# Attention value products in six blocks of an iteration (3, 3, 2, 3, 3 and 2 key tiles) where eight blocks of 2 stood

## The chip, the cores and the metric

One Trainium2 chip, one core. The metric is the device time of one execution in microseconds, as a median of runs. Every number of the profile is from one profiled execution of the kernel.

## The reference

A transformer block with conditioned normalisation, for two sequences of 2048 tokens of width 512, in fp32:

```python
xm = _modulate(_ln(x), sh_msa, sc_msa)
q = (xm @ Wq + bq).reshape(B, S, NH, DH)      # B=2, S=2048, NH=16 heads, DH=32
k = (xm @ Wk + bk).reshape(B, S, NH, DH)
v = (xm @ Wv + bv).reshape(B, S, NH, DH)
q = q / DH
w = jnp.einsum('bqhc,bkhc->bhqk', q, k)
w = jax.nn.softmax(w, axis=-1)
y = jnp.einsum('bhqk,bkhc->bqhc', w, v).reshape(B, S, H)
x = x + g_msa[:, None, :] * (y @ Wo + bo)
xm2 = _modulate(_ln(x), sh_mlp, sc_mlp)
h = jax.nn.gelu(xm2 @ W1 + b1, approximate=False)
x = x + g_mlp[:, None, :] * (h @ W2 + b2)
```

## The kernel before

The program has three stages one after another: `project` (normalisation, q, k and v), `attend` (L754, the attention) and `feed_forward` (L1334). The change touches `attend` and three functions ahead of it.

Attention runs in `N_IT` = 32 iterations. One iteration is a group of `HPG` = 4 heads of one sequence and 512 queries; it goes over `NKT` = 16 key tiles of 128 keys. A key tile holds four scores, one for each head, so that an iteration has 64 scores. The same work lies on five engines, and each works through its own queue in the order written in the program:

- TensorE: for each head of each key tile one score product (`scores`, L1213, 97 rows, output 128 x 512 into one of three `s_bank`s), and behind each score one product for the row maxima of the next iteration (`max_product`, L1197, L1205 in rows). In iteration 0 there is one more of these for every eight scores (`maxima_issued`, L694). After every second key tile t (`t % 2 == 1`) it runs one block of value products (`times_v`, L1224): tiles t-3 and t-2, four heads each, into the one `y_bank`. A score or maximum uses the whole width of the array; a value product is 128 x 32, four of them side by side. The array thus changes between the two kinds at both ends of every block. Behind the block after key tiles 3 and 11 stand the denominators of an eight-tile half (`sums`, L1240, of the same 128 x 32 kind). At score 46, once an iteration, the maxima found are transposed into a row (`max_transpose`, L1208).
- VectorE: one reduction for every maximum product (`maximum`, L1075, L1078 in rows), then `negative` (L1080) and `as_row` (L1084) once an iteration.
- ScalarE: one exponential for every score (L1054) into `probs`, a ring of `RING` = 5 key tiles. Ahead of a tile's first exponential it waits in `slot_free` (L1035) until the value products of the tile five back are done, and until GpSimd has added up that tile's pair. `take_sum` (L987) copies the denominators out of their bank, `take_y` (L981) the value result.
- GpSimd: adds the probabilities of two tiles each (`first_pair`, L903, `second_pair`, L908) and issues the DMAs that fold them (`fold_quad`, `fold_half`).
- SyncE: loads keys, queries and values; `next_v` (L844) waits for the value products of a quarter before it loads the next group's.

The maximum products, the row and the denominators share one ring of four PSUM banks, handed out by `MaxRing` (L722) in the order of TensorE's queue. A product into a bank waits for the reader of what was there four uses before:

```python
            self.bank[use], self.count[use] = at % self.BANKS, counts[reader]
            after.append((reader, counts[reader]))
            self.free_after[use] = after[at - self.BANKS] if at >= self.BANKS else None
```

Likewise a score waits until the exponential three scores before it is done.

Of the kernel before, what the change touches and what calls it, by code (L numbers as in the profile page):

```python
# [18 lines left out]
HPG = P // DH  # L19
# [5 lines left out]
NKT = S // P  # L25
# [5 lines left out]
N_IT = B * G * BPB  # L31
N_MAX = BPB * HPG * TT
CHUNK = TOK // P
N_SC = HPG * NKT
N_TILES = N_IT * NKT
N_BLOCKS = N_TILES // 2
N_QUADS = N_TILES // 4
QPI = NKT // 4
LAST_QUAD = N_QUADS - QPI
# [2 lines left out]
LAST_HALF = LAST_QUAD // HALF_QUADS  # L42
# [11 lines left out]
class Space:  # L54


    def __init__(self, nc, ctx, name):
        self.parts = ctx.enter_context(nc.sbuf_tensor(f"{name}_parts", [P, KT, TOK], F32R))

        size = KT * TOK * 4  # L60
        self.plain = nc.alloc_sbuf_tensor_at(f"{name}_plain", [P, KT, TOK], F32, offset=nc.sbuf_base - size)
# [638 lines left out]
def maxima_at(i, s):  # L700

    return [(1 + g // N_MAX, g % N_MAX) for g in range(maxima_issued(i, s), maxima_issued(i, s + 1)) if 1 + g // N_MAX < N_IT]
# [4 lines left out]
    return i + 1 < N_IT and maxima_issued(i, s) <= N_MAX * (i + 1) + BEFORE - 1 < maxima_issued(i, s + 1)  # L707


def due_sums(b):  # L710

    if b >= N_BLOCKS - 3:
        first = LAST_HALF + b - (N_BLOCKS - 3)
        return (first - 1, first) if first == LAST_HALF else (first,)
    return ((b - 9) // 4,) if b >= 9 and b % 4 == 1 else ()


class MaxRing:  # L722
# [4 lines left out]
    def __init__(self):  # L727
        uses = []
        for i in range(N_IT):
            for s in range(N_SC):  # L730
                uses += [("max", j, n) for j, n in maxima_at(i, s)]
                if row_at(i, s):
                    uses.append(("row", i + 1))
                b, within = divmod(N_SC * i + s, 2 * HPG)
                if within == 2 * HPG - 1:
                    uses += [("sum", u) for u in due_sums(b) if u <= LAST_HALF]
        self.bank, self.count, self.free_after = {}, {}, {}
        counts = {"vector": 0, "scalar": 0}
        after = []
        for at, use in enumerate(uses):  # L740
            reader = "scalar" if use[0] == "sum" else "vector"
            counts[reader] += 1
# [3 lines that stand above are left out]
# [8 lines left out]
def attend(nc, sh, late, feed, x, Wo, W1, W2):  # L754
# [7 lines left out]
    with ExitStack() as ctx:  # L762
# [216 lines left out]
        @block.scalar  # L979
        def _(act):  # L980
            def take_y(i):  # L981
                act.wait_ge(av_done, NKT * (i + 1))
                if i >= 2:
                    act.wait_ge(y_stored, 16 * (i - 1))
                act.activation(y_buf[:, i % 2, :], y_bank[:, :], ACT.Copy).then_inc(y_taken, 1)

            def take_sum(h):  # L987
                act.wait_ge(d_done, h + 1)
                if h >= HPI and h % HPI == 0:
                    act.wait_ge(d_moved, 16 * h)  # L990
                act.activation(d_raw[:, h % HPI, :], m_bank[ring.bank["sum", h]][:, :], ACT.Copy).then_inc(d_taken, 1)

            def take_last_sums():
                act.wait_ge(d_done, LAST_HALF + QPI)
                act.wait_ge(d_moved, 16 * LAST_HALF)
                act.activation(d_raw[:, 0, :], m_bank[ring.bank["sum", LAST_HALF]][:, :], ACT.Copy).then_inc(d_taken, 1)

            def move_sums(i):
                act.wait_ge(d_taken, HPI * (i + 1))
                if i:  # L1000
                    act.wait_ge(small_ready, i)
                for q in range(HPI):
                    act.dma_start(d_small[:, q, :], d_raw[0:P:DH, q, :]).then_inc(d_moved, 16)

            def store_inv(i):
                act.wait_ge(small_ready, i + 1)
                if i:
                    act.wait_ge(inv_in, 16 * i)
                act.dma_start(sh.inv_rows, inv_small[:, :]).then_inc(inv_stored, 16)

            def load_inv(i):
                act.wait_ge(inv_stored, 16 * (i + 1))
                if i:
                    act.wait_ge(y_normed, i)
                act.dma_start(inv[:, :], sh.inv_rows.rearrange("h (a n) -> h a n", a=1).broadcast_to([HPG, DH, TOK])).then_inc(inv_in, 16)

            def store_y(i):
                group, tok = i // BPB, i % BPB * TOK
                act.wait_ge(y_normed, i + 1)
                act.dma_start(sh.y_cols[group, :, tok:tok + TOK], y_buf[:, i % 2, :]).then_inc(y_stored, 16)  # L1020

            def wo_high(t):
                act.wait_ge(feed.wo_in, 16)
                act.activation(feed.wo_hi[:, t, :], feed.wo_raw[:, t, :], ACT.Copy).then_inc(feed.wo_hi_ready, 1)

            def round_first_y(g):
                act.wait_ge(feed.y_in[g], 16)
                act.activation(feed.first_y_hi[:, g, :], feed.first_y[:, g, :], ACT.Identity, bias=sh.vecs[:, ROW_BV + g:ROW_BV + g + 1])

            def bias_first_y(g):  # L1030
                act.activation(feed.first_y[:, g, :], feed.first_y[:, g, :], ACT.Identity, bias=sh.vecs[:, ROW_BV + g:ROW_BV + g + 1]).then_inc(feed.y_biased, 1)

            SPARE = (7, 9, 11, 15)

            def slot_free(tile):  # L1035
                c, r = tile // 4, tile % 4
                act.wait_ge(av_done, tile + 1)
                if r == 0:
                    act.wait_ge(*firsts(c))
                if r == 2:  # L1040
                    act.wait_ge(second_ready, 2 * c + 2)

            for i in range(N_IT):
                for t in range(NKT):
                    tile = NKT * i + t
                    if t == 2 and i:
                        take_y(i - 1)
                    if tile >= 20 and tile % 8 == 4 and (tile - 20) // 8 < LAST_HALF:
                        take_sum((tile - 20) // 8)
                    for h in range(HPG):  # L1050
                        act.wait_ge(s_done, HPG * tile + h + 1)
                        if h == 0 and tile >= RING:
                            slot_free(tile - RING)
                        act.activation(probs[:, tile % RING, h, :], s_bank[(HPG * tile + h) % 3][:, :], ACT.Exp).then_inc(p_done, 1)  # L1054
                    if i >= 2:
                        if t == 1:
                            store_inv(i - 2)
                        if t == 5:
                            load_inv(i - 2)
                        if t == 13:  # L1060
                            store_y(i - 2)
                    if i and t == 13:
                        move_sums(i - 1)
                    if i == N_IT - 4 and t in SPARE:
                        wo_high(SPARE.index(t))
                    if i == N_IT - 3 and t in SPARE:
                        round_first_y(SPARE.index(t))
                    if i == N_IT - 2 and t in (3, 7, 9, 11):
                        bias_first_y((3, 7, 9, 11).index(t))
            take_y(N_IT - 1)  # L1070
            take_last_sums()
# [119 lines left out]
        def _(pe):  # L1191
# [114 lines left out]
            for i in range(N_IT):  # L1306
                pe.wait_ge(row_in[i % 2], 16 * (i // 2 + 1))
                for t in range(NKT):
                    for h in range(HPG):
                        scores(i, t, h)  # L1310
                        for j, n in maxima_at(i, HPG * t + h):
                            max_product(j, n)
                        if row_at(i, HPG * t + h):
                            max_transpose(i + 1)
                        n = N_SC * i + HPG * t + h - OUT_FROM
                        if 0 <= n < len(OUT_ORDER):
                            first_out(n)
                    if i == N_IT - 1 and t in (11, 13):
                        first_transposes(t - 11)
                        first_transposes(t - 10)  # L1320
                    if t % 2 == 1:
                        b = (NKT * i + t) // 2
                        if b:
                            times_v(2 * b - 2)
                            times_v(2 * b - 1)
                        for u in due_sums(b):
                            sums(u)
            first_up()
            times_v(N_TILES - 2)
            times_v(N_TILES - 1)  # L1330
# [438 lines left out]
```

## Time and profile before

| | us |
|---|---|
| median of 3 runs (2729.82, 2737.03, 2735.59) | 2735.59 |
| the profiled execution | 2730.14 |
| its span, first to last instruction | 2728.0 |
| attention: first score to last value product | 345.7 to 1920.4 |

Over the span TensorE is busy 2690.0 us, VectorE 2007.5, GpSimd 1870.5 and ScalarE 1341.3. Matmuls overlap in the array and their ends are modelled, so TensorE's busy time isn't a measure of how well it is used: the starts of its instructions are. In the rows below a line of the timeline is one or several like instructions in a row, with the time of the first start, the time to the end of the last, and in brackets the idle time of the engine ahead of them. A value product is recorded as two matmuls, so that `x16` is two key tiles.

### The profile page before, as it was taken

The numbers are of one execution on the slowest core, as the hardware profiler recorded it, in microseconds if no ns is written. First come the engines' busy times: TensorE is split into PE (matmuls) and PEld (weight loads), VectorE is DVE, ScalarE is ACT, GpSimd is POOL, SyncE is SP. The second block draws the span as 40 slices with busy tenths as digits, with TensorE's granted clock in tenths as the row PEclk, the third lists the DMA queues.
The fourth block names the chain that finished last, engine by engine and source line by source line (L and its number), as shares of the span: only waits on it lengthen the run. The fifth ranks groups of instructions, "written<-read, shape, count | busy, mean of one in ns | idle before, by whom it ended". The sixth has DMA issues, their size and how long they took to land. (4 is left out here: it accounts for less than half of the span.)

```text
span 2728.0 us, 37942 instructions
## 1 busy us (share of the span) xinstructions
PE 2690.0 (99%) x13737; PEld 1780.1 (65%) x13737; DVE 2007.5 (74%) x3326; ACT 1341.3 (49%) x2534; POOL 1870.5 (69%) x1083
## 2 busy tenths in 40 slices
PE   7999999999999999999999999999999999999998
PEld 5777755555555555555555555554788888888887
DVE  6557688888888888888888888887675765765754
ACT  2322267676676766767667676776221221221211
POOL 1000088989989999998999989897655455555553
PEclk9999999999999999999999999999999999999999
DMA  6555458788888879878888888875410110110000
GB/s 247 204 186 165 159 128 176 167 185 179 178 182 174 187 167 189 182 166 185 178 179 184 174 186 170 198 166 121 147 41 11 47 46 2 47 47 1 31 16 16
DMA packets 143754, 369.22 MB, mean 135 GB/s; under 512 B 23572, under 2 KB 40528, under 8 KB 119760
## 3 DMA queue, kind: packets, MB, share of 16 engines
q0 software_dynamic: 26784, 195.05, 35.8%
q1 hardware_dynamic: 96000, 155.26, 19.0%
q10 hardware_dynamic: 20784, 16.49, 2.1%
q8 instruction: 110, 1.80, 0.3%
q14 instruction: 76, 0.62, 0.1%
HBM read 111.97 MB, written 58.97 MB: 63 GB/s over the span
## 5 line engine op out<-in xcount | busy, mean ns | idle before, releaser
L1078 DVE TENSOR_REDUCE part_max<-shared_bank 128x1 f32<-128x512 f32 x1972 | 1207.3, 680 | 274.2 <-PE shared_bank L1205 274.1
L1054 ACT ACTIVATE probs<-s_bank 128x512 f32<-128x512 f32 x2048 | 1034.3, 627 | 289.0 <-PE s_bank L1221 285.2
L1232 PE MATMUL y_bank<-probs,vs 128*32 128x512 f32 x4096 | 493.2, 599 | 0.0
L905 POOL TENSOR_TENSOR first_sum<-probs 128x1024 f32<-128x1024 f32 x124 | 343.5, 2771 | 78.4 <-ACT probs L1054 78.3
L1655 ACT ACTIVATE h<-shared_bank,vecs 128x512 f32<-128x512 f32 x128 | 88.1, 688 | 562.9 <-PE shared_bank L1679 558.0
L1221 PE MATMUL s_bank<-late_parts 97*128 97x512 f32 x848 | 349.3, 413 | 2.5 <-ACT probs L1054 2.5
L905 POOL TENSOR_TENSOR half_sum<-probs 128x1024 f32<-128x1024 f32 x124 | 336.9, 2733 | 14.7 <-ACT probs L1054 14.6
L1205 PE MATMUL shared_bank<-late_parts 96*128 96x512 f32 x848 | 336.6, 397 | 0.9
L916 POOL TENSOR_TENSOR wo<-probs 128x1024 f32<-128x1024 f32 x124 | 335.0, 3063 | 0.4 <-ACT probs L1054 0.4
L916 POOL TENSOR_TENSOR second_sum<-probs 128x1024 f32<-128x1024 f32 x128 | 317.8, 2625 | 13.4 <-ACT probs L1054 6.4
L1465 POOL TENSOR_TENSOR late_parts<-w_raw,late_parts 128x512 fp32r<-128x512 f32 x96 | 129.2, 1346 | 226.3 <-DVE late_parts L1542 226.3
L1232 PEld LDWEIGHTS y_bank<-probs,vs 128*32 128x32 f32 x4096 | 106.9, 109 | 241.4 <-issue 121.7
L1221 PEld LDWEIGHTS s_bank<-late_parts 97*128 97x128 f32 x848 | 160.0, 189 | 133.5 <-issue 88.0
L1552 DVE CAST h_hi<-h 128x512 fp32r<-128x512 f32 x128 | 79.7, 623 | 179.2 <-ACT h L1655 179.1
L1677 PE MATMUL acc_bank<-w_hi,h_hi 128*128 128x512 f32 x512 | 201.4, 393 | 1.4 <-DVE h_lo L1554 1.3
L1677 PE MATMUL shared_bank<-late_parts 128*128 128x512 f32 x508 | 201.2, 396 | 1.1 <-PEq L762 1.1
L1679 PE MATMUL acc_bank<-w_hi,h_lo 128*128 128x512 f32 x512 | 200.8, 392 | 0.0
L1679 PE MATMUL shared_bank<-late_parts 128*128 128x512 f32 x508 | 199.3, 392 | 0.0
L1678 PE MATMUL acc_bank<-w_lo,h_hi 128*128 128x512 f32 x512 | 199.0, 389 | 0.0
L1678 PE MATMUL shared_bank<-late_parts 128*128 128x512 f32 x508 | 198.8, 391 | 0.0
L1205 PEld LDWEIGHTS shared_bank<-late_parts 96*128 96x128 f32 x848 | 161.4, 190 | 30.5 <-DVE part_max L1078 5.4
L1221 PE MATMUL s_bank<-space_parts,late_parts 97*128 97x512 f32 x432 | 177.7, 412 | 0.0
(199 smaller groups left out, 4566.8 us busy)
## 6 DMA issues: line engine op xcount, KB each, us to landing
half_sum<-second_sum POOLq DMA_DIRECT2D x62, 1024.0 KB, 13.5
first_sum<-wo POOLq DMA_DIRECT2D x62, 1024.0 KB, 10.0
half_sum<-first_sum POOLq DMA_DIRECT2D x62, 1024.0 KB, 7.6
late_plain<-in_x SPq DMA_DIRECT2D x16, 1024.0 KB, 7.0
q_parts<-qk_out SPq DMA_DIRECT2D x32, 512.0 KB, 3.1
k_parts<-qk_out SPq DMA_DIRECT2D x32, 512.0 KB, 3.4
late_parts<-q_parts SPq DMA_DIRECT2D x63, 256.0 KB, 11.4
late_parts<-k_parts SPq DMA_DIRECT2D x60, 256.0 KB, 11.8
```

Source lines behind the costliest of these rows:

```text
L905: pool.tensor_tensor(first_home(c)[:, hs, :], probs[:, 4 * c % RING, hs, :], probs[:, (4 * c + 1) % RING, hs, :], ALU.add).then_inc(first_ ...
L916: pool.tensor_tensor(second_home(c)[:, hs, :], probs[:, (4 * c + 2) % RING, hs, :], probs[:, (4 * c + 3) % RING, hs, :], ALU.add).then_inc ...
L1054: act.activation(probs[:, tile % RING, h, :], s_bank[(HPG * tile + h) % 3][:, :], ACT.Exp).then_inc(p_done, 1)
L1078: v.tensor_reduce(part_max[:, i % 2, hs, c:c + 1], m_bank[ring.bank["max", i, n]][:, :], AX.X, ALU.max).then_inc(m_taken, 1)
L1205: pe.matmul(m_bank[ring.bank["max", i, n]][:, :], queries[i % 3][0:STACK, h, s * P:(s + 1) * P], keys[u][0:STACK, h, :], start=True, stop= ...
L1221: pe.matmul(s_bank[n % 3][:, :], keys[u][0:STACK + 1, h, s * P:(s + 1) * P], queries[i % 3][0:STACK + 1, h, :], start=True, stop=True).the ...
L1232: last = pe.matmul(y_bank[h * DH:(h + 1) * DH, :], vs[:, t, h * DH:(h + 1) * DH], probs[:, tile % RING, h, :], start=(t == 0), stop=(t == ...
L1465: pool.tensor_tensor(feed.w1_lo(j), w1_raw[j * 4 // MT][:, :, j % (MT // 4) * P:(j % (MT // 4) + 1) * P], feed.w1_hi(j).bitcast(F32), ALU. ...
L1655: act.activation(h[:, j % 2, :], up_bank[j % 2][:, :], ACT.Gelu, bias=sh.vecs[:, ROW_B1 + j:ROW_B1 + j + 1]).then_inc(up_taken, 1)
L1677: pe.matmul(bank, hi_l, hi_r, start=first, stop=False)
L1678: pe.matmul(bank, hi_l, lo_r, start=False, stop=False)
L1679: return pe.matmul(bank, lo_l, hi_r, start=False, stop=last)
```

## The change

Value products are issued after the key tiles whose number less two is in `BLOCK_ENDS`, that is after tiles 4, 7, 9, 12 and 15 of an iteration and tile 1 of the next one, with 3, 3, 2, 3, 3 and 2 tiles a block. Before, it was after every odd tile, 2 tiles a block. The youngest tile of a block is two tiles back, as before. The last iteration keeps its blocks of two at the same places. The denominators stand behind the blocks after tiles 4 and 12 (before: 3 and 11), and ScalarE takes them ahead of the exponentials of tiles 5 and 13 (before: 4 and 12); `MaxRing` hands out the banks in that order. The last iteration keeps its denominators' places too.

```diff
-def due_sums(b):
-    if b >= N_BLOCKS - 3:
-        first = LAST_HALF + b - (N_BLOCKS - 3)
-        return (first - 1, first) if first == LAST_HALF else (first,)
-    return ((b - 9) // 4,) if b >= 9 and b % 4 == 1 else ()
+BLOCK_ENDS = (2, 5, 7, 10, 13, 15)
+
+def value_tiles(tile):
+    i, t = divmod(tile - 2, NKT)
+    if i == N_IT - 1:
+        return (tile - 3, tile - 2) if t % 2 == 1 else ()
+    if i < 0 or t not in BLOCK_ENDS:
+        return ()
+    at = BLOCK_ENDS.index(t)
+    first = BLOCK_ENDS[at - 1] + 1 if at else 0
+    return range(NKT * i + first, NKT * i + t + 1)
+
+def due_sums(tile):
+    i, t = divmod(tile, NKT)
+    if i == N_IT - 1:
+        return {3: (LAST_HALF - 2,), 11: (LAST_HALF - 1, LAST_HALF), 13: (LAST_HALF + 1,), 15: (LAST_HALF + 2,)}.get(t, ())
+    return ((tile - 20) // 8,) if tile >= 20 and tile % 8 == 4 else ()
...
-                b, within = divmod(N_SC * i + s, 2 * HPG)
-                if within == 2 * HPG - 1:
-                    uses += [("sum", u) for u in due_sums(b) if u <= LAST_HALF]
+                if s % HPG == HPG - 1:
+                    uses += [("sum", u) for u in due_sums(NKT * i + s // HPG) if u <= LAST_HALF]
...
-                    if tile >= 20 and tile % 8 == 4 and (tile - 20) // 8 < LAST_HALF:
-                        take_sum((tile - 20) // 8)
+                    for u in due_sums(tile - 1) if tile else ():
+                        if u < LAST_HALF:
+                            take_sum(u)
...
-                    if t % 2 == 1:
-                        b = (NKT * i + t) // 2
-                        if b:
-                            times_v(2 * b - 2)
-                            times_v(2 * b - 1)
-                        for u in due_sums(b):
-                            sums(u)
+                    for tile in value_tiles(NKT * i + t):
+                        times_v(tile)
+                    for u in due_sums(NKT * i + t):
+                        sums(u)
```

## Rows read from the trace of the kernel before

**Rows 1.** The page: busy time, share of the span and instructions of each engine.
```profile
PE 2690.0 (99%) x13737; PEld 1780.1 (65%) x13737; DVE 2007.5 (74%) x3326; ACT 1341.3 (49%) x2534; POOL 1870.5 (69%) x1083
```
**Rows 2.** Iteration 14: window, length, busy (instructions) of PE, PEld, DVE, ACT, POOL.
```profile
1030.07:1078.78 48.71, 48.63 (x277) 27.33 (x274) 39.70 (x68) 33.78 (x67) 43.40 (x24) 1.00 0.88 185
```
**Rows 3.** Timeline of TensorE around one block of value products.
```profile
1003.18 0.39 PE L1205 MATMUL shared_bank<-keys,late_parts 96*128 96x512 f32 x1
1003.50 1.92 PE L1232 MATMUL y_bank<-probs,vs 128*32 128x512 f32 x16
1005.35 0.50 PE L1221 MATMUL s_bank<-late_parts 97*128 97x512 f32 x1
1005.69 0.39 PE L1205 MATMUL shared_bank<-keys,late_parts 96*128 96x512 f32 x1
...
1008.94 0.40 PE L1205 MATMUL shared_bank<-keys,late_parts 96*128 96x512 f32 x1
```
**Rows 4.** Timeline of TensorE around a block with denominators behind it.
```profile
1036.20 0.40 PE L1205 MATMUL shared_bank<-late_parts,space_parts 96*128 96x512 f32 x1
...
1039.48 0.39 PE L1205 MATMUL shared_bank<-late_parts,space_parts 96*128 96x512 f32 x1
1039.80 1.92 PE L1232 MATMUL y_bank<-probs,vs 128*32 128x512 f32 x16
...
1042.51 0.50 PE L1221 MATMUL s_bank<-late_parts 97*128 97x512 f32 x1
```
**Rows 5.** Timeline of VectorE: the eight reductions behind the block of rows 3.
```profile
1006.12 4.88 DVE L1078 TENSOR_REDUCE part_max<-shared_bank 128x1 f32<-128x512 f32 x8 [0.92 <-PE shared_bank L1205]
```
**Rows 6.** Timeline of TensorE's weight loads at the end of that block.
```profile
1005.35 0.19 PEld L1221 LDWEIGHTS s_bank<-late_parts 97*128 97x128 f32 x1 [0.84 <-issue]
1005.46 0.19 PEld L1205 LDWEIGHTS shared_bank<-keys,late_parts 96*128 96x128 f32 x1
```
**Rows 7.** Timeline of all engines, a stretch of iteration 0 with nine maxima.
```profile
360.19 5.47 DVE L1078 TENSOR_REDUCE part_max<-shared_bank 128x1 f32<-128x512 f32 x9 [0.71 <-PE shared_bank L1205]
...
363.02 0.81 PE L1205 MATMUL shared_bank<-late_parts 96*128 96x512 f32 x2
363.32 0.19 PEld L1205 LDWEIGHTS shared_bank<-late_parts 96*128 96x128 f32 x1 [0.34 <-DVE part_max L1078]
363.76 0.16 PEld L1232 LDWEIGHTS y_bank<-probs,vs 128*32 128x32 f32 x8 [0.25 <-ACT probs L1054]
```
**Rows 8.** Timeline of all engines around the row of maxima, end of key tile 11.
```profile
1014.55 1.88 DVE L1078 TENSOR_REDUCE part_max<-shared_bank 128x1 f32<-128x512 f32 x3
...
1014.72 0.48 PE L1221 MATMUL s_bank<-late_parts 97*128 97x512 f32 x1
1015.28 0.19 PEld L1205 LDWEIGHTS shared_bank<-late_parts,space_parts 96*128 96x128 f32 x1 [0.40 <-DVE part_max L1078]
...
1016.34 0.27 DVE L1088 CAST neg_max_row<-shared_bank 16x128 fp32r<-16x128 f32 x1
1016.54 0.67 DVE L1078 TENSOR_REDUCE part_max<-shared_bank 128x1 f32<-128x512 f32 x1
```
**Rows 9.** Timelines of GpSimd and of ScalarE, iteration 10: pair 4, 5; tiles 8, 9.
```profile
857.68 3.06 POOL L905 TENSOR_TENSOR first_sum<-probs 128x1024 f32<-128x1024 f32 x1
...
859.74 4.03 ACT L1054 ACTIVATE probs<-s_bank 128x512 f32<-128x512 f32 x8 [1.77 <-PE s_bank L1221]
```
**Rows 10.** Who waited for whom in the whole span, with times and longest.
```profile
PEld s_bank L1221 <- issue: 212.1, 253, 0.8
...
PEld shared_bank L1205 <- DVE part_max L1078: 14.8, 39, 0.4
```
**Rows 11.** The same for ScalarE alone, from 394 us to 1870 us.
```profile
ACT probs L1054 <- POOL first_sum L905: 0.9, 1, 0.9
```

More of the change, by code:

```diff
@@ L35 @@
 N_TILES = N_IT * NKT
-N_BLOCKS = N_TILES // 2
 N_QUADS = N_TILES // 4
```

## The prediction

> **What bounds the kernel now.** I read the page first, for how much each engine has to do: TensorE is busy 99% of the span, VectorE 74%, GpSimd 69%, ScalarE 49% [rows 1]. Then one iteration by itself, since the change alters 31 of the 32 alike: of 48.71 us TensorE is busy 48.63, GpSimd 43.40, VectorE 39.70, ScalarE 33.78, all at the full granted clock [rows 2]. TensorE carries the end, and every other engine has some room on the average. But the change leaves the averages nearly alone and alters the order in time, so the timelines decide.
>
> The first thing to see in them is what a block of value products costs besides its products. From the last maximum ahead of a block to the first one behind it are 2.51 us, 1003.18 to 1005.69 [rows 3]. A step between two scores or maxima is 3.25 / 14 = 0.232 us there and 3.28 / 14 = 0.234 in the other stretch [rows 3, 4]; I take 0.2335. With the denominators (one key tile's worth of the same products) last maximum to next score takes 1042.51 - 1039.48 = 3.03 us, against 1005.35 - 1003.18 = 2.17 without [rows 3, 4], so a tile is 0.86 us, and the denominators pay for no change of their own. Of the 2.51 us, 2 x 0.2335 are steps and 2 x 0.86 are products: 0.33 us is the price of turning the array to the narrow products and back. It shows as a gap of 0.84 us ahead of a score's weight load [rows 6], 253 times in the waits [rows 10], some eight times an iteration.
>
> The second thing is VectorE between two blocks. It takes a reduction every (4.88 - 1.88) / 5 = 0.600 us, 0.68 us each [rows 5, 8], while TensorE makes a maximum every 0.467 us. It loses 0.133 us per maximum and makes it good during the value products; its 0.92 us idle ahead of the next eight [rows 5] shows that it does.
>
> **What the change removes.** Two turns of the array in each of iterations 0 to 30: 62 x 0.33 = -20.5 us. The same 16 value tiles and two denominators are made, at 0.86 us each, in both orders. Before and after, the denominators share a turn with value products. This is on TensorE's path and comes off whole, if nothing else is late.
>
> **What it adds: runs of 12 maxima where runs of 8 stood.** The runs between blocks become 12, 12, 8, 12, 12 and 8 (tiles 2-4, 5-7, 8-9, 10-12, 13-15, 0-1). The ring of four banks lets a maximum start only when the reduction of the one four before is over. Let a run start at 0 with its first score (1005.35). Its first maximum is at 0.34 and the k-th after it at 0.34 + 0.467k [rows 3]; its weight load, where nothing holds it, starts one step earlier, at 0.11 + 0.467k (1005.46 for the first [rows 6]). The reductions start at 0.77 (1006.12) and the k-th ends at 1.45 + 0.60k [rows 5]. The load of maximum k+4 is free about 0.05 us later: in iteration 0, where a run has nine maxima, the fifth reduction ends at 360.19 + 4 x 0.599 + 0.68 = 363.27 and the ninth maximum's load starts at 363.32 [rows 7].
>
> So the eighth maximum (k = 7) could be loaded at 3.38 and is free at 1.45 + 1.80 + 0.05 = 3.30. Runs of eight fit by 0.08 us, and that is why the waits show VectorE holding such a load 39 times only [rows 10]: 30 rows of maxima and nine in iteration 0. The ninth is free at 3.90 and wants 3.84, and each further one is 0.133 later. A late load isn't hidden: from 363.32 to the block behind are 0.44 us, from an unhindered maximum 0.32 [rows 3, 7], and a score behind a gap comes 0.34 before the next instead of 0.2335 [rows 3], so some 0.11 us of it shows. The twelfth (k = 11) therefore starts at 1.45 + 0.60 x 7 + 0.05 + 0.11 = 5.81 instead of 0.34 + 5.14 = 5.48. **A run of 12 is 0.33 us longer**: exactly what a saved turn gives back. The small delays of the ninth to eleventh are contained in it, for the last one alone sets when the block starts. There are three such runs.
>
> The fourth, tiles 10 to 12, has the row of maxima in it. Up to its eighth maximum, which today already waits (load at 1015.28 [rows 8]), nothing changes. Behind it: the next score streams at 1015.28 + 0.11 + 0.23 = 1015.62, and its maximum must wait for the second of the three reductions from 1014.55, which ends at 1014.55 + 0.60 + 0.68 = 1015.83: with 0.05 and 0.11 that is 1015.99, where 1015.86 was possible. The next waits for the third, 1016.43 + 0.16 = 1016.59 instead of 1016.46. The last two wait for the copy of the row, over at 1016.61, and for the reduction over at 1017.21 [rows 8], and both are in time. Together 0.26 us.
>
> Sum of an iteration: 3 x 0.33 + 0.26 - 2 x 0.33 = **+0.58 us**. Iterations 1 to 29: +16.8. Iteration 0 has 13, 14, 13 and 14 maxima in the long runs, nine in the two short ones. By the same terms a run of nine loses 0.17 (4.01 against 3.84), one of 13 loses 6.41 - 5.71 = 0.70, one of 14 loses 1.07. Eight nines lose 1.4 now; four long runs and two nines 3.9 after: +2.5 - 0.66 = +1.8. In iteration 30 the maxima end at key tile 10, so only two long runs are late: 0.66 - 0.66 = 0. The last iteration keeps its blocks. In all +18.6 us on the profiled execution's own 2730.1 (span 2728.0): 2748.7. The profiled execution was 5.5 us under the median of the runs; on the median the sum is 2735.6 + 18.6 = **2754.2 us**.
>
> **Moved steps, costed at nothing.** ScalarE's scores ring of three banks: its eight exponentials take 4.03 us [rows 9], 0.50 apart at most against 0.467, so a run of 12 costs it 0.4 us of lead at most, while the maxima's waits give TensorE's scores as much back. `take_sum` moves one tile later with its denominators, still directly behind them; the DMA of the denominators (tile 13) comes behind it as before. `slot_free` wants the value products of five tiles back: with a block after tile 4 tile 5 finds tile 0 done, since its score stands behind that block on TensorE anyway. On SyncE's queue `next_v` waits for tile 3's and tile 11's products, two tiles later each; the first row load stands behind tile 7's products, whose block (after tile 9) doesn't move. Those loads have most of an iteration. GpSimd: the pair of tiles 4 and 5 must be added before tile 9's exponentials. In iteration 10 it ends at 860.74 and tile 9 begins at 859.74 + 4 x 0.467 = 861.61, 0.9 us later [rows 9]; this is one of the closest, and held up by a fold's DMA that starts with tile 1 and so moves with tile 1. Where nothing holds it the room is about 2.8 us and shrinks by 0.8. It held ScalarE once for 0.9 us in 30 iterations [rows 11]. Bound: 0 to +3 us in all; I take 0.
>
> **Bounds of the added cost.** With the release lag at nothing a run of 12 loses 0.28, with 0.10 it loses 0.38; with a period of 0.595 it loses 0.30, 0.605 gives 0.37. Four runs in 30 iterations: 0.05 us each way is 6 us. A turn may be 0.31 to 0.35, 1.2 us each way. So +11 to +26, and the runs shown spread over 7 us.
>
> **The rivals.**
> (a) *Turns saved and nothing late*: 2735.6 - 20.5 = 2715 us. For it speaks that VectorE idles in every iteration [rows 2, 5]. Against it are the waits of rows 7 and 8, where the ring holds TensorE already with one maximum more than eight. The Trainium skill ("TensorEngine Tiling (Array Packing)", Key Properties) says that a change of tiling mode drains the engine; by that rule alone fewer blocks are all gain. The same page (Performance Considerations, PSUM Bottleneck) says that tiling speeds up TensorE but not the emptying of PSUM, which may become the bottleneck; that speaks for my forecast, and rows 7 show it. Chance 0.08.
> (b) *A draw*: the late loads cost about half of what I work out (the exposed 0.11 us already lies in the turn behind the run, so that a run loses 0.22 and the one with the row 0.15): 3 x 0.22 + 0.15 - 0.66 = +0.15 us an iteration, +5 us, 2740; with the low bounds above 0 or a little below. Against it is the 0.44 us of rows 7, which contains the entry to the block. Chance 0.14.
> (c) *GpSimd becomes late too*: its pair decides where its room, 0.9 us at the closest, falls under 0. If that came to 1 us in every iteration, 31 us more: about 2785. Against it the rows 9 and 11. Chance 0.04.
> (d) *A turn is not saved*: a block of three pays its third tile's own 0.33, and only the waits are added: 2735.6 + 18.6 + 20.5 = 2775. The denominators' 0.86 us as a third tile [rows 4] speak against it. Chance 0.03.
> The forecast has 0.71.
>
> **How the numbers follow.** About 0.3%, 8 us, is what a measurement of this kernel can tell from no change. The likeliest case gives 2754, with its bounds 2747 to 2762 on the median; a spread of some 5 us between medians of three runs makes that 2741 to 2767, which also holds part of the draw and leaves under 0.2 outside. Slower has the forecast, (c) and (d): 0.78. Within 0.3%: 0.14. Faster: 0.08.
>
> **What would show it.** In the windows an iteration takes 49.3 us. The block of three lasts 2.71 us from its first product to the next score, with the denominators 3.57. In the waits, the weight load of the maxima held by VectorE rises from 39 to several hundred (three or four in each long run), and the gap of 0.84 us falls from 253 to about 190. The twelfth maximum of an undisturbed run starts its load 5.70 us after the run's first score. I am wrong if an iteration is 48.1 us (a), or if ScalarE waits for GpSimd dozens of times (c).

## The result, and the profile after

| | before | after |
|---|---|---|
| median of the runs, us | 2735.55 (4 runs, 2729.82 to 2737.03) | 2772.14 (4 runs, 2770.53 to 2774.76) |
| ratio, 95% interval | | 1.014 (1.0124 to 1.0156) |
| profiled execution, us | 2730.14 | 2771.92 |
| its span, us | 2728.0 | 2769.8 |

The change makes the kernel 1.4% slower, where 0.7% slower (+18.6 us) was forecast. By the medians the loss is 36.6 us, by the two profiled executions 41.8, since the one of the kernel before was 5.5 us under its median. The sign and one mechanism were right, and about half of the loss wasn't in the sum. The page of the changed kernel, busy time by engine (as rows 1), then its iteration 14 (as rows 2: window, length, busy time of PE, PEld, DVE, ACT and POOL):

```profile
PE 2709.2 (98%) x13737; PEld 1763.9 (64%) x13737; DVE 2003.3 (72%) x3326; ACT 1350.2 (49%) x2534; POOL 1868.0 (67%) x1083
```
```profile
1050.29:1100.30 50.01, 49.23 (x277) 26.93 (x273) 39.59 (x68) 34.06 (x67) 44.24 (x24) 1.00 0.88 185
```

No engine has more to do. An iteration takes 50.01 us instead of 48.71, and TensorE now stands still for 0.8 us of it. To place the 41.8 us that the two spans differ by, the same stretches of both: iteration 0, iterations 1 to 29 together, iteration 30. First the kernel before, then the changed one.

```profile
345.68:396.76 51.08, 50.99 (x249) 30.37 (x250) 44.70 (x74) 33.85 (x65) 46.26 (x25) 0.93 0.53 114
...
396.76:1810.58 1413.82, 1410.26 (x7922) 793.07 (x7918) 1150.68 (x1971) 984.11 (x1951) 1283.27 (x670) 1.00 0.84 179
...
1810.58:1858.73 48.15, 47.75 (x274) 26.60 (x270) 34.32 (x51) 36.17 (x71) 47.11 (x26) 1.00 0.77 168
```
```profile
347.34:399.74 52.40, 51.68 (x249) 27.83 (x249) 44.25 (x74) 35.38 (x65) 45.66 (x25) 0.97 0.51 110
...
399.75:1850.71 1450.96, 1427.28 (x7921) 779.93 (x7917) 1147.83 (x1970) 991.65 (x1951) 1284.48 (x670) 1.00 0.83 174
...
1850.71:1903.08 52.37, 49.98 (x273) 26.88 (x269) 34.61 (x51) 36.46 (x71) 45.39 (x25) 0.97 0.70 153
```

| stretch | forecast, us | measured, us |
|---|---|---|
| ahead of the first score (345.68 to 347.34) | 0 | +1.7 |
| iteration 0 | +1.8 | +1.3 |
| iterations 1 to 29 | +16.8 (0.58 each) | +37.1 (1.28 each) |
| iteration 30 | 0 | +4.2 |
| the rest | 0 | -2.5 |

The 1.7 us ahead of the first score aren't the change's. The execution of the changed kernel has 3.4 us at half clock in the first stage, and that of the kernel before hasn't (the changed one, then the one before; the number ahead of the DMA's two is the granted clock):

```profile
40.50:43.90 3.40, 3.40 (x13) 3.01 (x14) 3.29 (x7) 2.00 (x4) 0.00 (x0) 0.50 0.35 130
...
40.50:43.90 3.40, 3.40 (x20) 2.83 (x19) 3.26 (x8) 2.10 (x4) 0.00 (x0) 1.00 0.37 141
```

Of the runs further on, e2, e8 and e9 have the same spell and their first score at 346.98, 347.34 and 347.52 us; e4 and e7 haven't, and are at 345.49 and 345.99.

The open question is thus 0.70 us in each of 29 iterations. The runs between the blocks answer where. This is the timeline of the changed kernel's run of tiles 2 to 4 in iteration 14, TensorE, its weight loads and VectorE, as rows 3, 5 and 7:

```profile
1056.09 0.50 PE L1239 MATMUL s_bank<-late_parts 97*128 97x512 f32 x1
...
1056.87 7.27 DVE L1096 TENSOR_REDUCE part_max<-shared_bank 128x1 f32<-128x512 f32 x12 [0.60 <-PE shared_bank L1223]
...
1061.80 0.19 PEld L1223 LDWEIGHTS shared_bank<-late_parts,space_parts 96*128 96x128 f32 x1 [0.30 <-DVE part_max L1096]
1062.22 0.16 PEld L1250 LDWEIGHTS y_bank<-probs,vs 128*32 128x32 f32 x8 [0.24 <-issue]
```

The twelfth maximum's load starts 1061.80 - 1056.09 = 5.71 us behind the first score; 5.70 was forecast. The reductions are (7.27 - 0.68) / 11 = 0.599 us apart. From first score to block the run takes 6.13 or 6.14 us in each of iterations 1 to 29, where an unhindered one would take 5.48 + 0.32 = 5.80. The run 5 to 7 takes 6.14 (once 6.21), the run with the row 6.73 instead of 4.59 for its eight. The two kinds of delay that were worked out are there, at their sizes. The run of tiles 13 to 15 is another matter: 6.88 us, 1.08 more than unhindered. TensorE in it, iteration 14:

```profile
1090.72 0.50 PE L1239 MATMUL s_bank<-late_parts,keys 97*128 97x512 f32 x1
...
1093.88 0.39 PE L1223 MATMUL shared_bank<-space_parts,late_parts 96*128 96x512 f32 x1
1094.96 0.50 PE L1239 MATMUL s_bank<-late_parts,keys 97*128 97x512 f32 x1 [0.69 <-ACT probs L1072]
...
1097.59 2.78 PE L1250 MATMUL y_bank<-probs,vs 128*32 128x512 f32 x24
```

One score starts 1.08 us behind the product ahead of it, 0.85 more than a step, for ScalarE. It is the last of tile 14, and by the ring of three score banks it waits for the exponential of the first of tile 14. ScalarE's own timeline tells why that one is late:

```profile
1091.35 1.57 ACT L1072 ACTIVATE probs<-s_bank 128x512 f32<-128x512 f32 x3
1092.67 0.32 ACTq L1037 DMA_DIRECT2D y_cols<-y_buf  x1
1092.78 0.63 ACT L1072 ACTIVATE probs<-s_bank 128x512 f32<-128x512 f32 x1
1093.08 1.13 ACTq L1020 DMA_DIRECT2D d_small<-d_raw  x2
1094.31 4.03 ACT L1072 ACTIVATE probs<-s_bank 128x512 f32<-128x512 f32 x8 [0.90 <-PE s_bank L1239]
```

Behind tile 13's exponentials its queue issues three DMAs (`store_y` and the two of `move_sums`, "if t == 13"), 0.32 and 1.13 us; the store's issue and the start of the others still lie under the last exponential. From 1093.41 to 1094.31 no exponential runs, though their scores are long there. The bracket names TensorE as the releaser, which had been done; by the order of the rows, what held ScalarE is the issuing row above it, and e1, e2 and e9 test that. Before the change the same issues stood ahead of a block of value products:

```profile
1022.26 0.32 ACTq L1020 DMA_DIRECT2D y_cols<-y_buf  x1
...
1022.68 1.13 ACTq L1003 DMA_DIRECT2D d_small<-d_raw  x2
1024.77 4.03 ACT L1054 ACTIVATE probs<-s_bank 128x512 f32<-128x512 f32 x8 [1.69 <-PE s_bank L1221]
```

They were over at 1023.81, about a microsecond before the next score gave ScalarE anything to do.

Iteration 30 has the same kind of loss once more, behind key tile 11, where `bias_first_y` has its last operation. The first product of the output projection (L1302, behind the first score of tile 12) needs it, and a block no longer stands between. TensorE idles 1.12 us, and its granted clock, full until then, is at 0.50 (1.2 GHz) in the next 3.4 us. The timeline and the window:

```profile
1886.58 0.47 PE L1302 MATMUL shared_bank<-space_parts,late_parts 128*128 128x512 f32 x1 [1.12 <-ACT late_plain L1048]
```
```profile
1887.10:1890.50 3.40, 3.40 (x14) 1.72 (x16) 3.40 (x1) 1.79 (x3) 3.40 (x2) 0.50 0.39 77
```

The kernel before had such a window in its last iteration, 1902.2 to 1905.6 at 0.50, and the changed one hasn't; part of the 2.5 us given back there lies in that. The stall doesn't settle whether the clock falls: e9 has it too, in the same place and of the same 1.12 us, and its clock stays at 1.00 behind it. Its product and window:

```profile
1864.76 0.47 PE L1303 MATMUL shared_bank<-space_parts,late_parts 128*128 128x512 f32 x1 [1.12 <-ACT late_plain L1051]
```
```profile
1865.20:1868.60 3.40, 3.40 (x27) 1.50 (x29) 3.40 (x1) 1.57 (x3) 3.40 (x2) 1.00 0.63 161
```

The waits of the whole span: the ring of the maxima held a load 39 times before and does 207 times now (several hundred was forecast; e9, with the issues out of the way, has 288); the gap ahead of a score behind a block fell from 253 to 191 times (about 190 was forecast). Not forecast is the growth of the second row below, scores held by exponentials: 239 times and 80.3 us, where it was 25 times and 11.8 us before.

```profile
PEld s_bank L1239 <- issue: 160.1, 191, 0.8
...
PEld s_bank L1239 <- ACT probs L1072: 80.3, 239, 1.3
PEld shared_bank L1223 <- DVE part_max L1096: 60.8, 207, 0.4
```

### The profile page after: what moved, and what is told of

It reads as the page before. It is cut to its first block and busy times, and to the rows that moved or that the text cites. A ratio compares the mean times of both kernels' runs of the same rounds, so it can differ in the third digit from the quotient of the medians.

```text
span 2769.8 us, 37942 instructions
## 1 busy us (share of the span) xinstructions
PE 2709.2 (98%) x13737; PEld 1763.9 (64%) x13737; DVE 2003.3 (72%) x3326; ACT 1350.2 (49%) x2534; POOL 1868.0 (67%) x1083
## 5 line engine op out<-in xcount | busy, mean ns | idle before, releaser
L1250 PE MATMUL y_bank<-probs,vs 128*32 128x512 f32 x4096 | 480.2, 597 | 0.0
L922 POOL TENSOR_TENSOR first_sum<-probs 128x1024 f32<-128x1024 f32 x124 | 335.2, 2703 | 146.2 <-ACT probs L1072 146.2
L922 POOL TENSOR_TENSOR half_sum<-probs 128x1024 f32<-128x1024 f32 x124 | 345.5, 2794 | 10.5 <-ACT probs L1072 10.4
L1223 PE MATMUL shared_bank<-late_parts 96*128 96x512 f32 x848 | 346.6, 409 | 1.0
L1250 PEld LDWEIGHTS y_bank<-probs,vs 128*32 128x32 f32 x4096 | 113.3, 109 | 253.4 <-issue 196.7
```

The lines of the kernel that those rows point to most:

```text
L922: pool.tensor_tensor(first_home(c)[:, hs, :], probs[:, 4 * c % RING, hs, :], probs[:, (4 * c + 1) % RING, hs, :], ALU.add).then_inc(first_ ...
L1223: pe.matmul(m_bank[ring.bank["max", i, n]][:, :], queries[i % 3][0:STACK, h, s * P:(s + 1) * P], keys[u][0:STACK, h, :], start=True, stop= ...
L1250: last = pe.matmul(y_bank[h * DH:(h + 1) * DH, :], vs[:, t, h * DH:(h + 1) * DH], probs[:, tile % RING, h, :], start=(t == 0), stop=(t == ...
```

## The experiments

**e1, the issues behind tile 15.** Theory: ScalarE's issues (the store and the move of the denominators) are the missing 0.75 us. Rival: the ring of the maxima or GpSimd makes the run 13 to 15 long.

```diff
-                        if t == 13:
+                        if t == 15:
                             store_y(i - 2)
-                    if i and t == 13:
+                    if i and t == 15:
                         move_sums(i - 1)
```

> The changed kernel, with ScalarE's two DMA issues (the store of the normalised values and the move of the denominators) behind key tile 15 instead of 13. Theory: behind tile 13 they now stand inside a run of twelve scores, hold up the exponentials of tile 14 and through the three score banks TensorE; behind tile 15 a block of value products covers them. Then the run of tiles 13 to 15 falls from 6.88 us to the 6.14 of the other long runs, an iteration from 50.03 to 49.3 us, and the time from 2772 to about 2750. Rival, VectorE or GpSimd make that run long: nothing changes, 50.0 us an iteration, 2772.

Measured: the run 13 to 15 takes 6.12 to 6.14 us in iterations 1 to 29, as the theory has it, and iteration 1 takes 49.27 us. But the kernel takes 3164.58 us, 1.160 times the time of the kernel before (1.1581 to 1.1615). The waits, then iteration 1:

```profile
DVE d_total L1111 <- DMA d_small<-d_raw: 420.2, 31, 26.0
...
ACT y_buf L1002 <- DVE inv_small L1115: 392.9, 30, 20.5
```
```profile
399.16:448.43 49.27, 49.16 (x277) 27.24 (x273) 39.20 (x66) 33.89 (x67) 41.59 (x23) 1.00 0.75 154
```

VectorE waits for the moved denominators at score 3 of the next iteration (`invert_small`), up to 26 us, its reductions stand in the queue behind, and the ring holds TensorE. ScalarE stands as well, since the store of the reciprocals behind tile 1 of its queue waits for them (the second row). In the kernel before, VectorE's wait was 1.8 us in all. A part of the loss is the clock: the mean granted clock of this execution is 0.934, against 0.998 in the kernel before beside it. The issue can't simply go where a block covers it: what it moves is due. The time of this run says nothing about the question; the runs and the iteration free of the new wait do.

**e2, the same cost in the kernel before.** The same issues behind key tile 12, inside a run of two tiles (`13` replaced by `12` in the lines of e1's diff).

> The kernel before, with the same two issues behind key tile 12 instead of 13, so that they stand inside a run of two tiles instead of ahead of a block. Theory: the fourth score of tile 13 waits about 0.8 us for the exponential of the first, the run 12 to 13 goes from 3.94 to 4.8 us, an iteration from 48.72 to 49.5 and the time from 2735 to about 2760. Rival, the issues cost nothing in any place: 48.72 and 2735.

Measured: ratio 1.0116 (1.0101 to 1.0131), 2760.71 us; the run 12 to 13 takes 4.95 us in most iterations (mean 4.99) instead of 3.94, an iteration 49.75:

```profile
1083.74 1.13 ACTq L1003 DMA_DIRECT2D d_small<-d_raw  x2
1085.00 2.07 ACT L1054 ACTIVATE probs<-s_bank 128x512 f32<-128x512 f32 x4 [0.94 <-PE s_bank L1221]
```
```profile
1085.65 0.50 PE L1221 MATMUL s_bank<-late_parts,keys 97*128 97x512 f32 x1 [0.69 <-ACT probs L1054]
```

The same three kinds of rows as in the changed kernel, without any change of blocks or maxima: the issues inside a run cost 1.0 us an iteration. That is more than the 0.8 expected. In the changed kernel they make the run 1.08 us longer than unhindered too, and 0.33 us of that lies over the delay that the ring of the maxima would cause by itself, so that they add 0.75 there. How it divides between the store and the move wasn't tried.

**e3 and e4, reductions of half the length.** They take VectorE's lag away, to see what the blocks do alone; half of the keys is left out of the maxima. e3 is e1's kernel, e4 the one before, both with this edit:

```diff
-                v.tensor_reduce(part_max[...], m_bank[...][:, :], AX.X, ALU.max)
+                v.tensor_reduce(part_max[...], m_bank[...][:, 0:TOK // 2], AX.X, ALU.max)
```

> The kernel of e1, with each of VectorE's reductions of the maxima over 256 of the 512 columns; the other half of the keys is left out of the maxima. Theory: the reductions then keep up with the maxima, the long runs lose their 0.34 us each, and what is left of the change is the saved turns: 2 x 0.33 us an iteration less than the kernel of e4, about 47.7 against 48.4 us. Rival, the exponentials (0.48 to 0.49 us apart against 0.467) hold the long runs: they stay 6.14 us and an iteration stays within 0.3 us of e1's 49.3.

> The kernel before with the same half reductions (256 of 512 columns, half of the keys left out of the maxima), as the counterpart of e3. Both theories: the runs of eight stay at 3.93 to 3.96 us; only the one with the row of maxima shortens from 4.59 by some 0.3 us, an iteration from 48.72 to about 48.4, the time to about 2726.

Measured: e3 takes 3118.12 us, for e1's reason, and only its runs can be used: 5-7 at 5.95, 10-12 at 5.97 and 13-15 at 5.88 us where e1's were 6.13, 6.73 and 6.13. e4: ratio 0.9955 (0.9939 to 0.9972), an iteration at 48.24 us, all of it from the run with the row of maxima: 4.06 us instead of 4.59. So the ring and VectorE's lag make the long runs longer, by 0.18 to 0.25 us more than the exponentials would by themselves (6.13 - 5.95 and 6.13 - 5.88).

**e5, e6: SyncE issues the move.** The way to free ScalarE without a late landing of the denominators. `move_sums` itself is moved to SyncE's program as it is; e6 has the half reductions besides.

```diff
                 load_row(i + 1)
+                if i:
+                    move_sums(i - 1)
...
-                        if t == 13:
+                        if t == 15:
                             store_y(i - 2)
-                    if i and t == 13:
-                        move_sums(i - 1)
```

> The changed kernel with both issues out of ScalarE's way without a later landing: SyncE issues the move of the denominators, behind the row's load and as soon as they are taken (key tile 13), and ScalarE stores the normalised values behind tile 15. In e1 the move behind tile 15 landed too late for the reciprocals at score 3, which held VectorE and then everything; its iteration 1, in which no reciprocals are due, took 49.27 us. Theory (the issues were the 0.75 us an iteration that the sum had missed; late landing was all that was wrong in e1): run 13 to 15 at 6.13 us, every iteration at 49.3, the time 0.56 us x 30 = 17 us above the kernel before and 22 below the changed one. Rival (the maxima's ring or GpSimd lengthen that run in the steady state): 50.0 us.

> The kernel of e5 with VectorE's reductions over 256 of the 512 columns, so that half of the keys is left out of the maxima. Against e4 (48.24 us an iteration). If VectorE's reductions are all that lengthens the long runs, an iteration is 0.67 us under e4's, 47.57 us. If the exponentials hold them for 0.1 to 0.15 us each, as e3's runs show, it is 47.75 to 47.9. If the turns saved are worth nothing, it is 48.2 or more. Time: 14 us under e4's by the middle case.

Measured: e5 1.062 (1.0599 to 1.0642), e6 1.0472 (1.0446 to 1.0497). The run 13 to 15 is at 6.13 us again, but the run 2 to 4 takes 11.5 us on average from iteration 3 on, with spells of half clock in most iterations (mean granted clock 0.969). The theory that only the denominators' landing was wrong in e1 fell. The wait is this one, and the DMA issues by line show the landing:

```profile
ACT y_buf L1012 <- DMA y_cols<-y_buf: 144.7, 29, 7.1
```
```profile
y_cols<-y_buf ACTq DMA_DIRECT2D x30, 256.0 KB, 12.2
```

The store of the normalised values, issued behind tile 15, lands 12.2 us later (2.3 us when it is issued behind tile 13), and `take_y` at tile 2 waits for it ahead of the exponentials. In the trace the three loads of the next queries, 256 KB each, are mostly issued within 2 us of it and land as late: at the store of 1151.54 us (13.3) they take 13.0, 13.9 and 13.8. The one store with no such loads beside it, in the last iteration, lands in 2.3. Whether sharing the DMA engines with them is the cause wasn't tried. e6's iteration 3, which escaped the wait, took 47.70 us, against the 48.24 of e4.

**e7, half of the change.** Seven blocks, of 3, 3, 2, 2, 2, 2 and 2 tiles, so that a block still follows tile 13.

```diff
-BLOCK_ENDS = (2, 5, 7, 10, 13, 15)
+BLOCK_ENDS = (2, 5, 7, 9, 11, 13, 15)
...
-    return ((tile - 20) // 8,) if tile >= 20 and tile % 8 == 4 else ()
+    return ((tile - 19) // 8,) if tile >= 20 and tile % 16 in (4, 11) else ()
```

> Half of the change: blocks of 3, 3, 2, 2, 2, 2 and 2 tiles, denominators behind tiles 4 and 11, so that only the runs 2 to 4 and 5 to 7 are long and a block still follows tile 13. Theory (a saved turn is worth 0.33, a run of twelve costs 0.34, an issue behind tile 13 is covered by the block behind it): -0.33 + 2 x 0.34 = +0.35 us, 49.07 us an iteration, 10 us over the kernel before. If turns counted alone: 48.4 us and 10 us under it. If the changed kernel's excess lay in any long run alike: 49.7.

Measured: 1.0024 (1.0014 to 1.0034), 2741.01 us against 2733.90. The mean of iterations 1 to 29 is 49.06 us, forecast 49.07. The two long runs take 6.13 and 6.14, the others are as before. Iteration 14:

```profile
1034.72:1083.82 49.10, 48.96 (x278) 27.36 (x274) 39.61 (x68) 33.74 (x67) 44.09 (x24) 1.00 0.89 186
```

This is the cleanest single test of the sum: one turn less (0.33), two long runs (2 x 0.34), no issue uncovered. It also speaks against the rival that any long run costs more (49.7). The time, +7.1 us, is a little under the 10 expected.

**e9 and e10, the change with both issues out of the way.** As e5 and e6, but `store_y` behind tile 12, which a block follows.

> The changed kernel with SyncE issuing the move of the denominators (as in e5) and ScalarE's store of the normalised values behind key tile 12 instead of 15. In e5 the move was in time, but the store behind tile 15 landed 12.2 us later instead of 2.3, and ScalarE waited 144.7 us for it ahead of the copy of the next values at tile 2. Behind tile 12 a block covers the issue and the landing has four tiles. Theory: all long runs take 6.13 to 6.14 us (6.73 with the row), every iteration 49.3 us instead of 50.03, and the time is 17 us (0.6%) above the kernel before. Rival (something else in the steady state lengthens run 13 to 15): 50.0 us and 1.4%.

> The kernel of e9 with VectorE's reductions over 256 of the 512 columns (half of the keys left out of the maxima), against e4. Theory: 48.24 - 0.67 for the turns, + 0.15, 0.15, 0.03 and 0.06 for what the exponentials hold in the four long runs as e3 and e6 show them: 47.9 us an iteration less the 0.1 to 0.2 that the short runs lose no more, so 47.7 to 47.9, and 10 to 16 us under e4's time. If the turns were worth nothing: 48.2 or more.

Measured: e9 1.0068 (1.0051 to 1.0085), 2749.50 us against 2730.44; e10 0.9914 (0.9897 to 0.9931), 2706.98 us. In e9 the long runs take 6.12 to 6.14 us (6.73 with the row), but for two of 6.40 and 6.21. First e9's iteration 14 and its waits, then e10's iteration 13 and e4's iteration 14:

```profile
1040.55:1089.83 49.28, 49.15 (x278) 27.22 (x274) 39.49 (x68) 33.95 (x67) 44.05 (x24) 1.00 0.89 188
```
```profile
PEld shared_bank L1224 <- DVE part_max L1097: 79.4, 288, 0.4
...
PEld s_bank L1240 <- ACT probs L1075: 24.2, 94, 2.0
```
```profile
967.97:1015.66 47.69, 47.69 (x277) 26.91 (x273) 27.50 (x68) 33.52 (x67) 43.78 (x24) 1.00 0.84 175
```
```profile
1021.66:1069.91 48.25, 48.25 (x278) 27.40 (x274) 27.49 (x68) 33.67 (x67) 42.95 (x24) 1.00 0.88 186
```

e9 is the kernel that the forecast had described: 49.28 us an iteration against 48.75 (means of iterations 1 to 29), +0.53, and +19 us in all. Scores held by exponentials fell from 239 waits to 94. And e10 against e4 is the change with neither ScalarE's issues nor VectorE's lag in its way: 0.56 us less in this pair of iterations. The turns saved (0.66) are real, less some 0.1 us that the exponentials take back in the long runs (run 5 to 7 at 5.92 us against 5.80 unhindered). Over iterations 1 to 29 the means are 47.89 and 48.24, 0.35 us apart, as the two ratios are (0.9914 and 0.9955, 0.4% or 11 us). Eight of e10's iterations take 0.3 to 1.4 us more than 47.7. Over the whole span ScalarE waits for GpSimd six times, 4.3 us, where e9 has no such row; ahead of the longest of these waits GpSimd waits for a fold's DMA:

```profile
ACT probs L1075 <- POOL first_sum L932: 4.3, 6, 1.1
```
```profile
1421.53 0.90 POOL L947 DMA_DIRECT2D half_sum<-first_sum  x1 [3.45 <-DMA first_sum<-wo]
...
1425.88 2.07 ACT L1075 ACTIVATE probs<-s_bank 128x512 f32<-128x512 f32 x4 [1.09 <-POOL first_sum L932]
```

At this pace the folds begin to count. Five of the six waits stand in a run 8 to 9, each behind a wait of GpSimd of 2.8 to 3.5 us for a fold's DMA. These runs are 3.2 us longer together than the others in their place, and iterations 1 to 29 together are 5.6 us longer than 29 times 47.7. No run takes the folds away to test it.

**e8, the row of maxima three scores later, in the kernel before.** e4 had shown what hangs on VectorE's lag there.

```diff
 def row_at(i, s):
+    before = 6 if i + 2 < N_IT else BEFORE
-    return i + 1 < N_IT and maxima_issued(i, s) <= N_MAX * (i + 1) + BEFORE - 1 < maxima_issued(i, s + 1)
+    return i + 1 < N_IT and maxima_issued(i, s) <= N_MAX * (i + 1) + before - 1 < maxima_issued(i, s + 1)
```

> The kernel before with its eight blocks, and the row of maxima transposed three scores later (score 49 instead of 46, behind the block after key tile 11; the last row stays at 46). e4 showed that the 0.66 us extra of the run 10 to 11 hang on VectorE's lag when the row is due. Theory: behind the block VectorE has caught up, the run 10 to 11 falls from 4.59 us to about 3.95 and the run 12 to 13 grows by the row's own 0.1 to 0.2: an iteration from 48.72 to 48.2 or 48.3, the time 13 to 16 us under the kernel before. Rival (the row's cost is its own, wherever it stands): 48.7 us, no change; or the row lands too late for the next iteration and it takes longer.

Measured: 0.9942 (0.9922 to 0.9961), 2721.46 us against 2733.90. The run 10 to 11 takes 3.95 us instead of 4.59, the run 12 to 13, which has the row now, 4.07. The timeline shows the row's product without a gap on either side, where rows 8 had one of 0.40 behind it (ahead of the next maximum's load), and the window is iteration 14:

```profile
1061.59 0.40 PE L1206 MATMUL shared_bank<-space_parts,late_parts 96*128 96x512 f32 x1
1061.83 0.27 PE L1212 MATMUL shared_bank<-ident,neg_max 128*16 128x128 f32 x1
1061.86 0.48 PE L1222 MATMUL s_bank<-late_parts,keys 97*128 97x512 f32 x1
1062.18 0.40 PE L1206 MATMUL shared_bank<-space_parts,late_parts 96*128 96x512 f32 x1
```
```profile
1024.32:1072.55 48.23, 48.23 (x278) 27.42 (x274) 39.70 (x68) 33.67 (x67) 43.06 (x24) 1.00 0.89 186
```

It is faster than both kernels, with the full computation and the eight blocks left as they were.

## Why the prediction was right or wrong

*Direction and mechanism: right.* Each long run loses what a saved turn gives. Forecast 0.33 and 0.26 us, measured 0.34, 0.34 and, for the run with the row, 6.73 - 4.59 = 2.14 against the 1.87 of four more scores and maxima: 0.27. e7 and e9 give the sum of an iteration as worked out (49.06 and 49.28 us), e10 shows what it is without VectorE's lag. That e9's 1.0068 is the 18.6 us forecast to the digit is in part luck: its iterations 1 to 29 give 15 us instead of 16.8, and misses of both signs in the other stretches make it up.

*What a turn costs: right.* 0.33 us; the block of three lasts 2.71 us and with denominators 3.57, as forecast.

*"Moved steps, costed at nothing": the step that failed.* It says of ScalarE's DMA issues that "the DMA of the denominators (tile 13) comes behind it as before". The issue's place in ScalarE's queue was as before, its cover wasn't: a block of value products followed tile 13, and after the change none does until tile 15. The 0.32 and 1.13 us of issuing were in the timeline of the kernel before, at 1022.26 and 1022.68, and no row of them was read. ScalarE's room in a run was put at 0.4 us of lead lost over twelve exponentials; against that, issuing for 1.1 us in the middle is a stall of TensorE of 0.85 us (1094.96 - 1093.88, less a step), and once it has come the scores follow at the exponentials' pace to the run's end. The run is 6.88 - 5.80 = 1.08 us longer than unhindered; net of the 0.33 in the sum it is 0.75 us an iteration, 22 us in 29 iterations. With the 18.6 that is 40.4 us of the 41.8 between the spans. That so little is left is partly luck: the 1.4 us are misses of both signs, +1.7 ahead of the first score, -0.5 in iteration 0, -1.5 in iterations 1 to 29, +4.2 in iteration 30 and -2.5 behind it. e2 finds the cost in the old order (1.0 us), e9 takes it out of the new one (49.28 us an iteration instead of 50.03).

*The same step, iteration 30.* Costed at 0, measured +4.2 us. It has one wait of TensorE for `bias_first_y`, behind the loss of the block after tile 11, then 3.4 us at half clock, and the issues behind tile 13 as in every iteration. e9 separates them, though it wasn't made for it: it has the same wait at the full clock and no issues in the run 13 to 15, and its iteration 30 takes 49.80 us instead of 52.37. Its run 10 to 12 takes 7.24 us against 8.24 and the block behind it 3.57 against 4.10, which is the half clock (1.5 us); its run 13 to 15 takes 5.85 against 6.88 (1.0 us). Of what is left over the kernel before, 49.80 - 48.15 = 1.65 us, most is the wait: the run 10 to 12 with it takes 7.24 us, the run 13 to 15, also without maxima but without a wait, 5.85. No run takes the wait away.

*Iteration 0:* forecast +1.8, measured +1.3 (52.40 us; e9's is 52.26). That stretch holds a spell of half clock in both kernels, 6.8 us in the one before and 3.4 in the changed one (0.93 against 0.97 granted), so its size can't be read as the ring's alone.

*The rivals.* (a), turns saved and nothing late, holds in part where the reductions are halved (e10, 0.35 us of the 0.66 as a mean), and not here. (b), a draw by a smaller delay: the delays were of full size. (c), GpSimd late: in the changed kernel's waits ScalarE's exponentials don't wait for it once; it begins with e10's pace of 47.7 us. (d), a turn not saved: e7 and e10 exclude it. The cause of the other half was none of them: it is in a third engine's queue, and reaches TensorE through the three score banks.

*Of the Trainium skill's two sentences* ("TensorEngine Tiling (Array Packing)"): that a change of tiling mode drains TensorE (Key Properties) agrees with the 0.33 us of a turn and with e10, whose iterations are shorter for two turns less. That emptying PSUM may become the bottleneck (PSUM Bottleneck) agrees with the runs at 6.13 us only in kind: the page speaks of products sped up by tiling, and the products held here are those of the full width.

## What to carry to other kernels

When a block of work on the busiest engine is merged with its neighbour, list what every other queue does in the gap that disappears, DMA issues included: each of them was hidden by it. A ring of few banks between a fast producer and a slower reader is judged by the longest run between two pauses, not by the average load: here eight maxima fitted by 0.08 us, each further one would have come 0.13 us later than wanted, and four of them made the run 0.33 us longer. And what is moved to a covered place must still land in time, for whoever waits for it at the far end.

## What the runs showed of the hardware that was not expected

Issuing two DMAs of 8 KB each from ScalarE's queue kept it from its next activation for about 0.9 us with the data ready (the rows 1093.08 to 1094.31). One and the same 256 KB store landed in 2.3 us behind tile 13, 4.3 behind tile 12 (e9) and 12.2 behind tile 15 (e5), as medians. And a stall of TensorE of 1.12 us in iteration 30 was followed by 3.4 us at a granted clock of 0.50 in the changed kernel, and by a clock that stayed at 1.00 in e9; those 3.4 us at 1.2 instead of 2.4 GHz cost about 1.5 us.
